# Routing the last row of a sine-attention and mixture-of-experts kernel: a fifth group in place of a dense pass

## The reference

```
x = x + Wo * attention(layernorm(x)),  attention = sin(30 * q.k / sqrt(8)) * v, 16 heads of 8
n = layernorm(x)
x = x + shared_expert(n) + sum over the 2 best of 8 experts e of score_e(n) * expert_e(n)
expert(n) = (silu(n @ Wg.T) * (n @ Wu.T)) @ Wd.T,  Wg, Wu: 256 x 128, Wd: 128 x 256
score = sigmoid(n @ Wr.T + rb)
```

## Time and profile before

| what | value |
|---|---|
| time, median of 3 runs (lowest, highest) | 492.1 us (491.87, 494.67) |
| the profiled execution's own time | 491.92 us |
| its span, first to last instruction | 490.0 us |
| mean granted TensorE clock over the span | 0.981 |
| PE, ACT, DVE, POOL busy | 87%, 70%, 60%, 49% |

### The profile page before, as it was taken

How to read it: one execution, slowest core, us unless ns; L and a number is a source line. 1 busy time by engine, 2 the same in 40 slices (tenths; PEclk the granted TensorE clock), 3 DMA queues, 4 the chain that set the end, 5 groups by cost and what they waited for, 6 DMA issues and landing times.

```text
span 490.0 us, 12316 instructions
## 1 busy us (share of the span) xinstructions
PE 427.6 (87%) x4432; PEld 224.0 (46%) x4432; DVE 292.0 (60%) x999; ACT 340.5 (70%) x470; POOL 238.6 (49%) x308
## 2 busy tenths in 40 slices
PE   2898899999978999899999998999999787978771
PEld 1321233323322445444554444444445776967761
DVE  6876685554723446578574666754654544547783
ACT  1668889878869986788688876777876453654540
POOL 5332450300565243228686854256856845567631
PEclk9999999999999999999999999999999978999996
DMA  5047589456046424962465349911122434431111
GB/s 166 2 132 207 117 245 328 91 159 166 18 128 178 98 56 123 185 121 70 132 189 127 70 135 191 167 55 55 50 61 56 104 98 111 113 98 44 50 50 32
DMA packets 82186, 56.05 MB, mean 114 GB/s; under 512 B 28752, under 2 KB 76496, under 8 KB 82128
## 3 DMA queue, kind: packets, MB, share of 16 engines
q1 hardware_dynamic: 77824, 47.74, 38.5%
q0 software_dynamic: 3584, 7.35, 5.6%
q10 hardware_dynamic: 720, 0.20, 0.2%
HBM read 22.62 MB, written 27.13 MB: 102 GB/s over the span
## 4 chain that ended last, share of the span: by engine, by line
PE 55%; issue 12%; DVE 11%; ACT 9%; another core or an unknown queue 3%; POOL 3%; DMA 3%; SPq 1%; ACTq 0%; DVEq 0%; POOLq 0%
PE o_ps L713 15%; PE score L700 8%; ACT attn L975 6%; PE tile_ps L840 4%; PE tile_ps L838 3%; PE tile_ps L839 3%; PE tile_ps L863 2%; DVE hid L1308 2%; ACT gate L996 2%; PE score L840 2%; DMA y_back<-in_wd 2%; PE r_ps L682 1%; PE score L838 1%; PE r_ps L669 1%
## 5 line engine op out<-in xcount | busy, mean ns | idle before, releaser
L975 ACT ACTIVATE attn<-score 128x1024 f32<-128x1024 f32 x256 | 248.5, 1025 | 31.3 <-PE score L700 26.2
L1532 POOL TENSOR_TENSOR hid_lo<-hid,hid_hi 128x256 f16<-128x256 f32 (+1 forms) x94 | 72.4, 771 | 157.8 <-DVE hid_hi L1316 125.2
L713 PE MATMUL o_ps<-attn,vals 128*32 128x512 f32 x1024 | 136.4, 604 | 0.8 <-ACT o_t L982 0.5
L700 PE MATMUL score<-queries,keys 64*128 64x512 f16 x512 | 83.3, 383 | 11.1 <-ACT attn L975 7.7
L1308 DVE SCALAR_TENSOR_TENSOR hid<-tile_ps,gate 128x256 f32<-128x256 f32 (+1 forms) x88 | 40.3, 458 | 55.6 <-ACT gate L996 44.7
L996 ACT ACTIVATE gate<-tile_ps 128x256 f32<-128x256 f32 (+1 forms) x88 | 36.4, 414 | 44.3 <-PE tile_ps L840 35.9
L838 PE MATMUL tile_ps<-xt,w_hi 128*128 128x128 f16 x244 | 43.9, 219 | 1.3 <-ACT y_sb L1008 0.7
L839 PE MATMUL tile_ps<-xt,w_hi 128*128 128x128 f16 x244 | 43.9, 219 | 0.8 <-issue 0.8
L840 PE MATMUL tile_ps<-xt,w_lo 128*128 128x128 f16 x244 | 43.9, 219 | 0.5 <-issue 0.5
L700 PEld LDWEIGHTS score<-queries,keys 64*128 64x128 f16 x512 | 18.5, 93 | 55.8 <-ACT attn L975 31.8
L863 PEld LDWEIGHTS tile_ps<-w_hi,hid_hi 128*128 128x128 f16 x152 | 14.7, 97 | 58.9 <-issue 53.2
(11 more groups left out here) (223 smaller groups left out, 993.6 us busy)
## 6 DMA issues: line engine op xcount, KB each, us to landing
q_four<-q_parts SPq DMA_DIRECT2D x14, 256.0 KB
queries<-q_four SPq DMA_DIRECT2D x14, 256.0 KB
k_four<-k_minus SPq DMA_DIRECT2D x14, 256.0 KB
keys<-k_four SPq DMA_DIRECT2D x14, 256.0 KB
y_sorted<-y_sb SPq DMA_DIRECT2D x52, 64.0 KB
x_sorted<-zeros SPq DMA_DIRECT2D x2, 1472.0 KB, 8.9
queries<-q_three SPq DMA_DIRECT2D x14, 192.0 KB
keys<-k_three SPq DMA_DIRECT2D x14, 192.0 KB
```

Of the source, the lines that this page charges most:

```text
L700: mm = pe.matmul(score[h][:, i, :], keys[b % 2][rows, 2 * j + h, kt * P:(kt + 1) * P], queries[b % 2][rows, 2 * j + h, :], start=True, sto ...
L713: mm = pe.matmul(o_ps[32 * i:32 * i + 32, :], vals[b % 2][:, kt, h:h + 32], attn[k % RING][:, i, :], start=(k == 0), stop=(k == UNITS - 1))
L975: act.activation(attn[k % RING][:, 2 * (u % 2):2 * (u % 2) + 2, :], score[u % 2][:, :, :], ACT.Sin, scale=SIN_SCALE).then_inc(sined, 1)
L1532: pool.tensor_tensor(cells(hid_lo, d), cells(hid, d), cells(hid_hi, d), ALU.subtract).then_inc(lo_by_pool, 1)
```

## The change

Row 7 becomes a fifth routed group, (7,), so its 16 FULL jobs go and 8 SPARSE jobs (15 tiles) come. Its steps `E_...` behind TAIL move: packing from +11, +13 to +9, +10, the choice of experts from +25 to +17, then `ranks` at +18, `parts` and `places` at +19, `tile_experts` at +21, `shares` at +27, scatters in +24 to +31. Behind TAIL there are now 30 jobs, 76 to 105: group 2 (+0 to +20), group 3 (+22 to +36), group 4 (+38 to +52), and last the shared tiles, row 6's at +54 and row 7's at +56 and +58. Gathers behind the scatters are no longer kept apart: group 2's are in +33 to +48, group 3's in +49 to +56, group 4's in +65 to +72, one in each slot. The combines come earlier: +16 and +28 for group 1 (were +19, +31), +45 and +53 for group 2 (+51, +63), +61 for group 3 (+73), +76 for group 4. DVE makes the low halves of jobs 77, 80, 83 and of 86 to 103, in all 21 of the 30; POOL makes those of 76, 78, 79, 81, 82, 84, 85, 104 and 105. From job 85 on `down` uses the bank `r_ps` in turn with `o_ps`. The first scatter of group 4 waits for the loads of group 2, because it writes the same `x_sorted`; the first `store_y` of group 4 waits for the gathers of group 2.

```diff
-E_COPYO, E_OUT, E_RES, E_POW2, E_APPLY2, E_XHI, E_XLO = 1, 4, 5, 6, 8, 11, 13
-E_XT2, E_COPYX2, E_ROUTE, E_LOGIT, E_TANH, E_TOP, E_CHOOSE = 16, 17, 20, 21, 21, 23, 25
+E_COPYO, E_OUT, E_RES, E_POW2, E_APPLY2, E_XHI, E_XLO = 1, 4, 5, 6, 7, 9, 10
+E_XT2, E_COPYX2, E_ROUTE, E_LOGIT, E_TANH, E_TOP, E_CHOOSE = 12, 13, 14, 15, 15, 16, 17
+E_PREFIX, E_DISPATCH, E_SCATTER = 18, 19, 24
...
-ROUTE_GROUPS = [(0, 1), (2, 3), (4, 5), (6,)]
-DENSE = 7
+ROUTE_GROUPS = [(0, 1), (2, 3), (4, 5), (6,), (7,)]
...
-        elif late:
-            jobs.append(late.pop(0))
-        elif a >= TAIL + E_TILES and dense:
-            jobs.append(dense.pop(0))
+        elif late and late[0][0] <= a:
+            jobs.append(late.pop(0)[1])
...
-        out.append("r" if a >= TAIL + E_CHOOSE + 4 and out[-1] == "o" else "o")
+        out.append("r" if a >= TAIL + E_DISPATCH + 4 and out[-1] == "o" else "o")
...
-            if not (near[2] or near[0] and near[1] or near[1] and near[3] or near[3] and near[4]):
+            if not (near[2] or a < TAIL + E_SCATTER - 1 and (near[0] and near[1] or near[1] and near[3] or near[3] and near[4])):
...
-        return last + 6
-    return max(last + 8, TAIL + 16) if last + 8 >= TAIL else last + 8
+        return last + 4
+    return max(last + 5, TAIL + 16) if last + 8 >= TAIL else last + 8
...
-LO_DVE = [d for d in HI_ACT if GU_SLOT[d] + 2 in _gathering or GATHER_SLOT[-1][-1] <= GU_SLOT[d] <= GATHER_SLOT[-1][-1] + 3]
+_moving = _gathering | {scatter_slot(g, k) for g in range(len(ROUTE_GROUPS)) for k in range(SCATTERS[g])}
+LO_DVE = [d for d in HI_ACT if GU_SLOT[d] + 2 in _moving and GU_SLOT[d] + 3 in _moving or GU_SLOT[d] >= TAIL + E_SCATTER and (GU_SLOT[d] + 2 in _moving or GU_SLOT[d] + 3 in _moving)]
...
-                    pe.wait_ge(logit_ready, ROWS)
+                    pe.wait_ge(pos_ready, len(ROUTE_GROUPS))
...
+                if tail == E_PREFIX:
+                    ranks(len(ROUTE_GROUPS) - 1)
...
+                if tail == E_DISPATCH:
+                    parts(len(ROUTE_GROUPS) - 1)
+                    places(len(ROUTE_GROUPS) - 1)
+                if tail == E_DISPATCH + 2:
+                    tile_experts(len(ROUTE_GROUPS) - 1)
+                if tail == E_DISPATCH + 8:
+                    shares(len(ROUTE_GROUPS) - 1)
...
+                    if g == len(ROUTE_GROUPS) - 1:
+                        for n, (group, _, _) in enumerate(LOADS):
+                            if group == g - 2:
+                                pool.wait_ge(xt_loaded[n % XT], 16 * (n // XT + 1))
```

More of the change, by code:

```diff
@@ L111, in scatter_slot @@
 def scatter_slot(g, k):
+    if ROUTE_GROUPS[g][-1] == ROWS - 1:
+        return TAIL + E_SCATTER + k
     return SLOTS * (ROUTE_GROUPS[g][-1] + 1) + S_SCATTER + k + k // 2
 SCATTERS = [2 * TT * len(rows) for rows in ROUTE_GROUPS]
-SHARED, SPARSE, FULL = "shared", "sparse", "full"
+SHARED, SPARSE = "shared", "sparse"
 def plan():
-    shared = [(SLOTS * (j + 1) + S_COPYX2 + 3, (SHARED, j, t, None, 1)) for j in range(ROWS - 1) for t in range(TT)]
-    sparse = [(scatter_slot(g, SCATTERS[g]) + 8, (SPARSE, g, i, None, 1)) for g in range(len(ROUTE_GROUPS)) for i in range(GTILES[g])]
+    shared = [(SLOTS * (j + 1) + (S_COPYX2 if j < ROWS - 1 else E_COPYX2) + 3, (SHARED, j, t, None, 1)) for j in range(ROWS) for t in range(TT)]
+    sparse = [(scatter_slot(g, SCATTERS[g]) + (8 if g < len(ROUTE_GROUPS) - 1 else 6), (SPARSE, g, i, None, 1)) for g in range(len(ROUTE_GROUPS)) for i in range(GTILES[g])]
     jobs, slots = [], []
@@ L139, in in_twos @@
         return out
-    sparse, late = in_twos(sparse), [job for _, job in in_twos(shared)]
-    dense = [(SHARED, DENSE, t, None, 2) for t in range(0, TT, 2)] + [(FULL, DENSE, t, e, 2) for t in range(0, TT, 2) for e in range(ROUTED)]
+    sparse, late = in_twos(sparse), in_twos(shared)
     a = TAIL
-    while sparse or late or dense:
+    while sparse or late:
         if sparse and sparse[0][0] <= a:
             jobs.append(sparse.pop(0)[1])
-        elif late:
-            jobs.append(late.pop(0))
-        elif a >= TAIL + E_TILES and dense:
-            jobs.append(dense.pop(0))
+        elif late and late[0][0] <= a:
+            jobs.append(late.pop(0)[1])
         else:
@@ L642, in _ @@
                     store_row(ROUTE_GROUPS[g][row], combined_rows(g, row))
-                for t in range(0, TT, 2):
-                    if D_SLOT[JOBS.index((FULL, DENSE, t, ROUTED - 1, 2))] == a:
-                        store_last(t)
-            sync.wait_ge(out_stored, 16 * (ROWS - 1 + TT // 2))
+            sync.wait_ge(out_stored, 16 * ROWS)
             sync.wait_ge(q_stored, 64 * (ROWS - 1))
@@ L786, in piece @@
                     return part[:, :, :].rearrange("p e n -> p (e n)")[:, bass.ds(place_of[row, t + m], P)]
-                return part[:, own(e + 1 if kind == FULL else 0), :]
+                return part[:, own(0), :]
             placed = set()
@@ L1332, in read_down @@
                 mine = x_all[:, (row * TT + t) * DM:(row * TT + t + n) * DM]
-                if kind == SHARED:
-                    dve.wait_ge(x1_done, row + 1)
-                    dve.scalar_tensor_tensor(out=mine, in0=here, scalar=DOWN_UNSCALE, in1=mine, op0=ALU.mult, op1=ALU.add).then_inc(d_read, 1)
-                    return
-                dve.wait_ge(weight_ready, ROWS)
-                wait_read(dve, JOBS.index((FULL, row, t, e - 1, 2) if e else (SHARED, row, t, None, 2)))
-                for m in range(2):
-                    ins = dve.scalar_tensor_tensor(out=x_tile(row, t + m), in0=here[:, m * DM:(m + 1) * DM], scalar=weight[len(ROUTE_GROUPS) % 2][:, t + m, e:e + 1],
-                                                   in1=x_tile(row, t + m), op0=ALU.mult, op1=ALU.add)
-                ins.then_inc(d_read, 1)
+                dve.wait_ge(x1_done, row + 1)
+                dve.scalar_tensor_tensor(out=mine, in0=here, scalar=DOWN_UNSCALE, in1=mine, op0=ALU.mult, op1=ALU.add).then_inc(d_read, 1)
             def combine(g, row, t, c):
```

11 lines of the change are left out of this document (3 added, 8 removed).

## The result

The changed kernel takes 507.9 us (median of 4 runs, 507.0 to 510.8) where the kernel before takes 492.9 in the same sitting: 1.032 of it, 95% interval 1.028 to 1.037. The forecast was 486.8, the range ended at 497; the time lies above it, and even above the rival that I had called slower (502).

A forecast was written before the change was run, and what follows sets the result against it. Behind TAIL, PE's jobs plus stalls beside moves, then POOL's gathers and closing DRAIN, were taken to set the end: 416.5, 24.2 bare, 10.8 stalls, then the tail to span 484.9, plus 1.9 gives 486.8 us; range 479 to 497.

The forecast's parts named there:

- the rival that I had called slower: POOL's tail moves: 31 us of unbroken scatters and gathers hold up the other engines' work; 502 us, chance 0.15.
- Stalls: I take three runs of four, 10.8 us: Jobs 88 to 100: 16 gathers and 8 scatters beside SPARSE jobs cost 10.8 us, between 4.8 and 21.6.
- silu of job 88 at 416.5 as before: Start of the sum behind TAIL: job 88's silu comes at 416.5 us, unchanged from the kernel before.
- the stream starves the queues: POOL's moves from 411 on: each four cost 3.6 us, 21.6 lost in place of 10.8; 502 us, chance 0.15.
- the bare price of a job: PE behind TAIL: a two-tile SPARSE job takes 2.10 us without stalls, a one-tile job 1.05.
- DVE's dispatch: Row 7's routing on DVE, +19 to +27: 3.7 us against two PE jobs, costing 0 (hidden) to 1.5 us; taken as 0.
- Late places: Row 7's sorted rows, due by +38: 8 us slack; if routing slips further, job 95 waits; 491 us, chance 0.08.
- Group 3's gathers: POOL behind group 2's combine: they wait for `y_back` until 453.2, then 8 gathers take 9.8 us, to 463.0.
- The DRAIN: Kernel end: GpSimd's closing instruction ends 9.2 us behind its last instruction, plus 0.3 to the end of the span.
- the fast rival: Tail: gathers cost little (480.8 us) and the closing DRAIN is shorter behind a DMA (477.7); about 479, chance 0.20.
- The path that the sum called covered: Behind the last gather: landing, 8 combines and store finish at 481.8, 3.1 us before the end, so cost nothing.
- The shared port: DVE low halves beside group 3's gathers: each of 8 lengthened 0.45 us, chain 3.6 us longer; 490.4, chance 0.12.

The follow-up runs named there:

- e3b_pauses: Changed kernel with a GpSimd subtraction after every fourth of the first 32 moves from the scatters on, in the 492 us sitting: 503.1 us.
- e5_plain_moves: Changed kernel with group 2's 16 gathers as plain DMAs of fixed places, not the routed rows, in the 492 us sitting: 490.8 us.
- e8_all_lows_dve: Changed kernel with all low halves of the tail on DVE, where the kernel before takes 468 us: 466.7 us, 0.995 of the kernel before.
- e1_half_lows_pool: Changed kernel with low halves of every second job from +24 on (88 to 102) on POOL again, in a 468 us sitting: 476.1 us.
- e1b_half_lows: Changed kernel with low halves of every second job from +24 on POOL again, in another 468 us sitting: 476.0 us.
- e3_pauses: Changed kernel with a GpSimd subtraction after every fourth of the first 32 moves from the scatters on, in a 468 us sitting: 476.1 us.
- e2d_stream: Kernel before with all low halves of +22 to +66 on DVE, its 24 gathers in one run, at 468: 467.2 to 467.5 us, 0.998.

## Why the prediction was wrong

By its own chain, predicted and then in the profile after: silu of job 88 416.5, **425.7**; silu of job 100 451.5, **471.2**; group 3's first gather 453.2, **474.0**; its last ends 463.0, **485.3**; low halves 465.6, **488.8**; group 4's last gather ends 475.4, **498.7**; end 484.9, **505.6**. Of the 20.7 us 19.7 come in ahead of job 100; behind it the chain takes 34.4 us against 33.4 as worked out, but that is in part luck (below).

**The step that failed is "Stalls: I take three runs of four, 10.8 us"**, and "silu of job 88 at 416.5 as before" with it. The stretch 88 to 100 was 24.2 bare and took 45.5, so 21.3 us of stalls, at the upper bound of 21.6; and 9.2 us had been lost ahead of job 88, beside the scatters, which I had charged behind it. The trace of before had a price of 3.6 us for four moves beside SPARSE jobs, 0.9 each. I charged only three of the six fours, 0.45 us for each of the 24 moves, on the ground that the stream would be over before the jobs were. It cost 1.0 to 1.1 us a move beside group 2's gathers, no less than in fours in the kernel before; `e3b_pauses`, with 0.5 to 0.75 there, speaks for the missing spaces as a part of it, its scatters' stretch does not. The rival at 0.15, *the stream starves the queues*, was right in its mechanism, 502 by the sum, and 6 us short.

**Right:** that stalls lie beside moves; that this, not PE, was the weak term; the bare price of a job behind the streams (460.06 to 473.24, six steps in 13.2 us, 2.2 each against 2.10); the gathers' 1.25 us; that the work removed (16 FULL jobs) is real: with short moves it gives 0.98. **DVE's dispatch, taken at 0 with 1.5 as a bound:** at 468 its two steps take 8.6 us, 4.4 to 5.4 over the bare price (4.2, or 3.15 with one of them at half), the slow combine's 1.7 included. **Late places:** I had 8 us of slack and a chance of 0.08. At 468, where the jobs come on time, job 95 does wait 3.4 us for its load and job 102, for the reason told above, 3.6; at 492 PE waits for no load behind the standstill, but with group 2's gathers plain (`e5_plain_moves`) it waits for one of group 4's, 2.9 us.

**Group 3's gathers** wait, as predicted, for the combine of group 2's first row. The row's bracket names a store (22.56 us), and by the profile it did land last, 0.2 us behind the combine; but the first gather follows that combine by 1.07 us in this profile (472.92 to 473.99) and by 1.07 at 468 (436.77 to 437.84), where SP had issued that store at 430.50, and in `e8_all_lows_dve` the row itself names the combine. The combine ends 1.7 us behind silu of job 100, the term of the sum; the 1.07 us wasn't in it.

**The DRAIN was wrong in kind.** I added 9.2 us to POOL's last instruction because that was the figure behind a low half. Behind a DMA it is 2.8 to 3.2, and the end follows the last store, as half of the fast rival had it ("the DRAIN behind a DMA is shorter than behind a computation"). The path that the sum called covered, landing, combines and store, was 6.4 us to SP's last wait and took 6.5 (498.7 to 505.2). So the end comes 6.9 us behind the last gather and not 9.5, and these 2.6 us nearly cancel 3.6 that the pieces ahead took more: 1.1 before group 3's first gather, 1.5 in its eight, 0.8 with the two low halves, 0.2 in group 4's. That the stretch came out right to 1 us is luck.

**A reading** was loose too: in the first window of the earlier trace rows not every other engine is idle, since DVE works 1.33 and POOL 2.40 of the 4 us.

**The shared port** (0.12): group 2's and 3's gathers are 0.94 us in nearly all rows, so that rival didn't happen; but the combine of 2.02 us beside a low half of POOL, in the profile at 468, has three fellows: in `e1_half_lows_pool`, `e1b_half_lows` and `e3_pauses` one combine each takes 1.77 to 1.86 us beside a subtraction of POOL. All four end 0.16 us behind it. The exclusive use of a shared port for a whole instruction, of which the Trainium skill's page "SBUF — State Buffer", section "SBUF: two separate sides", speaks, fits these rows. It costs some 1.5 us once in a run.

**Still open.** That the first standstill, too, goes with the indirect form is argued from the second: no run at 492 made the scatters plain. And what is slow at 492. By the rows it is not DMA work (share 0.19, 49 GB/s at 440 to 444), not the clock, and not a wait that the profile shows (PE stands on "issue"); it goes with the indirect form on POOL's queue. That the engines' instructions arrive late beside it would fit one matmul every 0.7 us. The page has DMA queues of the kind "instruction", but they carry one packet from 436 to 450 at 492 and two from 418 to 432 at 468, which shows neither a crowd nor a cause. Also open: what the kernel before pays at 492. Against `e2d_stream` at 468 the last sine activations start 5.7 us later (370.99 against 365.31), from there to job 84, beside group 1's gathers, it takes 7 us more, and the last 29 steps take 73.9 us (402.51 to 476.41) against 62.1, 12 us. Whether its moves are all that, plain moves at 492 would have told.

## What to carry to other kernels

Count the indirect moves that an edit adds, and ask whether they will stand in a row: at 492 each of 16 in a row cost the jobs 1.0 to 1.1 us, and 16 more of them, in longer rows, ate the 8 jobs that they saved. A price read from stalls in the trace may rise when an edit takes the spaces away; to charge less than the trace shows needs a row that says so. An end that hangs on a closing instruction must be priced by what will stand before it after the edit. And run the kernel before beside every variant: from sitting to sitting it moved by 24 us, more than the whole change.

## What the runs showed of the hardware

- The same kernel takes 468 us on three chips and 492 on another. Of the 24.5 us between the spans of `before` and `e2d_stream` 5.7 lie ahead of the last sine activations and 18.8 behind, 11.8 of them in the last 29 job steps.
- A run of 16 indirect DMAs from POOL, 1.25 us apart, can bring all other engines to a near halt (PE 8 matmuls in 4 us, ACT and DVE none), from 4 us behind its start to 4 us behind its end, on one chip (492) and not on another (468).
- A plain DMA from POOL holds it 0.53 us (16 in 8.55), an indirect one 1.25, and a quarter of the bytes doesn't shorten it.
- POOL's closing DRAIN is over 9.2 to 9.3 us behind POOL's last instruction where that is a subtraction (8 profiles) and 2.8 to 3.2 us where it is a DMA (12 profiles). The length of its own row (4.4 to 13.5 us) says little, since the row begins at or before the start of the last instruction.
- A VectorE combine of 0.35 us takes 1.77 to 2.02 us beside a subtraction of 1.17 us on POOL, and ends 0.16 us behind it (four rows).
